# Layer 0's own attention: inner values on both halves of the rows, queries and keys two tiles at a time

## The reference

```python
def _mlp(h, W1, b1, W2, b2):
    return jax.nn.relu(h @ W1.T + b1) @ W2.T + b2
# H, HKV, HD = (16, 4, 64); OH = 64 (width of the hidden layer)
# Wq1 (64, 256), Wq2 (1024, 64): 16 query heads of 64
# Wk1 (64, 256), Wk2 (256, 64): 4 key heads of 64, each for four query heads
# values: x @ Wv.T + bv; causal softmax; the output times Wo (256, 1024)
```

## Time and profile before

| | |
|---|---|
| median of three runs | 2268.53 us |
| time of the profiled execution | 2268.6 us |
| its span, first to last instruction | 2266.8 us |
| TensorE busy in the span | 2013.3 us, 89% |
| VectorE, ScalarE, GpSimd busy | 1339.4, 905.5, 562.2 us |
| mean granted TensorE clock | 0.869 |
| stage of the change | from 386.8 us to about 518 us |
| weights of layer 0's own attention (pack l0a) | 2176 KB, landed 19.4 us after the issue at 3.77 us |

### The profile page before, as it was taken

One profiled execution on the slowest core, in us unless ns is written; L12 is line 12 of the kernel. 1 busy time (PEld: TensorE's weight loads), 2 busy tenths in 40 slices (PEclk: granted clock), 3 DMA queues, 4 the chain that ended last, 5 costly groups with the idle time before them and its releaser, 6 DMA issues.

```text
span 2266.8 us, 57634 instructions
## 1 busy us (share of the span) xinstructions
PE 2013.3 (89%) x22720; PEld 1463.7 (65%) x22720; DVE 1339.4 (59%) x3551; ACT 905.5 (40%) x3432; POOL 562.2 (25%) x1360
## 2 busy tenths in 40 slices
PE   8999999999988898998978888998999999789844
PEld 4899998877566565567866655665644545556623
DVE  6677666765355787445645614886263220678787
ACT  2455554443146565202334523665211111346522
POOL 3566665222011000102345512331000000411111
PEclk9555555999999899899998988999999999889965
DMA  3000001004000001200020000000030000000000
GB/s 139 4 5 5 5 5 66 16 1 185 1 5 5 12 12 53 87 0 24 1 100 37 2 1 8 9 12 1 1 154 0 1 0 0 5 11 12 5 0 16
DMA packets 8026, 57.21 MB, mean 25 GB/s; under 512 B 793, under 2 KB 5249, under 8 KB 5985
## 3 DMA queue, kind: packets, MB, share of 16 engines
q1 hardware_dynamic: 7760, 53.54, 6.2%
HBM read 52.62 MB, written 0.92 MB: 24 GB/s over the span
## 4 chain that ended last, share of the span: by engine, by line
PE 68%; DVE 15%; ACT 7%; issue 6%; POOL 4%; DMA 1%; POOLq 0%; DVEq 0%; SPq 0%; ACTq 0%
PE banks L269 43%; PE banks L274 8%; PE banks L1390 6%; PE banks L963 3%; ACT memory L1011 2%; PE banks L989 2%; DVE memory L1492 2%; PE banks L1543 1%; ACT memory L1417 1%; POOL memory L1449 1%; ACT memory L1424 1%; DVE memory L2835 1%; DVE memory L1498 1%; DVE memory L1273 1%; ACT memory L1256 1%
## 5 line engine op out<-in xcount | busy, mean ns | idle before, releaser
L269 PE MATMUL banks<-memory 128*112 128x256 f32 (+8 forms) x4192 | 1126.1, 424 | 99.2 <-DVE memory L3540 21.8
L269 PEld LDWEIGHTS banks<-memory 128*128 128x128 f32 (+3 forms) x4192 | 699.3, 194 | 434.2 <-issue 279.8
L274 PE MATMUL banks<-memory 112*125 112x112 f32 (+3 forms) x2000 | 301.5, 283 | 75.4 <-DVE memory L850 25.7
L274 PEld LDWEIGHTS banks<-memory 112*125 112x125 f32 (+3 forms) x2000 | 234.7, 170 | 190.9 <-issue 99.5
L1390 PE MATMUL banks<-memory 128*128 128x8 bf16 (+2 forms) x10752 | 306.9, 174 | 14.1 <-DVE memory L1475 1.4
L1390 PEld LDWEIGHTS banks<-memory 128*128 128x128 bf16 x10752 | 295.8, 104 | 25.8 <-POOL memory L1449 23.6
L1011 ACT ACTIVATE memory<-banks,memory 112x375 f32<-112x375 f32 x384 | 215.5, 579 | 26.1 <-DVE memory L1049 26.0
L1049 DVE TENSOR_REDUCE memory<-banks 112x2 f32<-112x750 f32 x192 | 171.1, 934 | 39.2 <-PE banks L963 39.0
L1492 DVE TENSOR_REDUCE memory<-banks 128x48 f32<-128x192 f32 x448 | 122.0, 291 | 61.9 <-PE banks L1390 47.6
L1057 DVE COPY memory<-banks 125x448 f32<-125x448 f32 x192 | 117.0, 620 | 9.5 <-PE banks L274 5.1
L1571 ACT ACTIVATE memory<-memory 112x112 f32<-112x112 f32 x192 | 71.7, 374 | 89.0 <-DVE memory L1592 89.0
(11 more groups left out here) (240 smaller groups left out, 2471.8 us busy)
## 6 DMA issues: line engine op xcount, KB each, us to landing
memory<-in_l2x SPq DMA_DIRECT2D x1, 7680.0 KB, 21.5
memory<-in_l2f SPq DMA_DIRECT2D x1, 7168.0 KB, 20.0
memory<-in_l1f SPq DMA_DIRECT2D x1, 4617.0 KB, 14.5
memory<-in_ctxT SPq DMA_DIRECT2D x24, 187.5 KB
memory<-in_l2f SPq DMA_DIRECT2D x1, 4096.0 KB, 12.9
memory<-in_l3f SPq DMA_DIRECT2D x1, 3073.0 KB, 22.3
memory<-in_l2a SPq DMA_DIRECT2D x1, 3072.0 KB, 18.4
memory<-in_l0f SPq DMA_DIRECT2D x1, 2304.0 KB, 9.2
```

The costliest lines, as they stand in the source:

```text
L269: ins = self.nc.tensor.matmul(out, weights[i], acts[i], start=i == 0, stop=i == n - 1)
L274: return self.nc.tensor.transpose(out, in_, self.ident[0:n, 0:n])
```

## The change

The hidden layers are computed twice: `wq1`, `wk1` and their biases are laid out twice side by side, so that a "hid" matmul fills 128 partitions, with the same 64 values in the lower and in the upper half. The second matrices are split in two halves of their outputs; the first half lies on rows 0 to 63, the other on rows 64 to 127. Queries then take eight matmuls in a row, alternately on the two halves, into two banks; keys four matmuls in the same manner, into two banks. The second "queries" entry of the order goes away, "keys" goes into EVEN and "queries" into ODD. VectorE waits for both banks of a step at once, and takes keys out in two instructions where there was one. Signals for keys count two an item.

```diff
-    EVEN = (("turn", 0, 2), ("sc", 0, 1), ("max", 0, 1), ("exp", 0, 1), ("queries", 0, 0), ("values", 0, 2),
+    EVEN = (("turn", 0, 2), ("sc", 0, 1), ("max", 0, 1), ("exp", 0, 1), ("keys", 0, 0), ("values", 0, 2),
             ("inv", 0, 1), ("y", 0, 3))
-    ODD = (("turn", 1, 2), ("sc", 1, 1), ("max", 1, 1), ("exp", 1, 1), ("keys", 0, 0), ("values", 1, 2),
-           ("queries", 1, 0), ("v", 0, 0), ("hid", 0, -1), ("hid", 1, -1), ("inv", 1, 1))
+    ODD = (("turn", 1, 2), ("sc", 1, 1), ("max", 1, 1), ("exp", 1, 1), ("queries", 0, 0), ("values", 1, 2),
+           ("v", 0, 0), ("hid", 0, -1), ("hid", 1, -1), ("inv", 1, 1))
...
-            k.project(k.bank(bank, 64, S), [w[("wq1", "wk1")[i]][:, j, :] for j in range(KD)],
+            k.project(k.bank(bank, P, S), [w[("wq1", "wk1")[i]][:, j, :] for j in range(KD)],
                       [self.hs[:, i, j, b, :] for j in range(KD)]).then_inc(*s.hid_full.up())
         elif step == "queries":
             PE.wait_ge(*s.hid_ready(2 * b + 1))
-            bank = k.next_bank(("queries", b, i), s.q_ready(2 * b + i + 1))
+            banks = [k.next_bank(("queries", b, h), s.q_ready(2 * b + h + 1)) for h in range(2)]
             for t in range(4):
-                c = 4 * i + t
-                ins = PE.matmul(k.bank(bank, P, 4 * S)[:, t * S:(t + 1) * S], w["wq2"][0:64, c * P:(c + 1) * P],
-                                self.r1[:, 0, :], start=True, stop=True)
-            ins.then_inc(*s.q_full.up())
+                for h in range(2):
+                    rows = slice(64 * h, 64 * h + 64)
+                    ins = PE.matmul(k.bank(banks[h], P, 4 * S)[:, t * S:(t + 1) * S],
+                                    w["wq2"][rows, t * P:(t + 1) * P], self.r1[rows, 0, :], start=True, stop=True)
+                    if t == 3:
+                        ins.then_inc(*s.q_full.up())
         elif step == "keys":
             PE.wait_ge(*s.hid_ready(2 * b + 2))
-            bank = k.next_bank(("keys", b), s.k_ready(b + 1))
-            for t in range(4):
-                ins = PE.matmul(k.bank(bank, P, 4 * S)[:, t * S:(t + 1) * S], w["wk2"][0:64, t * P:(t + 1) * P],
-                                self.r1[:, 1, :], start=True, stop=True)
-            ins.then_inc(*s.k_full.up())
+            banks = [k.next_bank(("keys", b, h), s.k_ready(2 * b + h + 1)) for h in range(2)]
+            for t in range(2):
+                for h in range(2):
+                    rows = slice(64 * h, 64 * h + 64)
+                    ins = PE.matmul(k.bank(banks[h], P, 2 * S)[:, t * S:(t + 1) * S],
+                                    w["wk2"][rows, t * P:(t + 1) * P], self.r1[rows, 1, :], start=True, stop=True)
+                    if t == 1:
+                        ins.then_inc(*s.k_full.up())
...
+            V.wait_ge(*s.q_full(2 * b + 2))
+            for h in range(2):
+                ps = k.bank(k.at["queries", b, h], P, 4 * S).rearrange("p (t s) -> p t s", t=4)
+                V.scalar_tensor_tensor(out=self.q[b % 2][:, 4 * h:4 * h + 4, :], in0=ps, scalar=0.125,
+                                       in1=self.bq2s[:, 4 * h:4 * h + 4].unsqueeze(2).broadcast_to([P, 4, S]),
+                                       op0=ALU.mult, op1=ALU.add).then_inc(*s.q_ready.up())
+        elif step == "keys":
+            if b >= 2:
+                V.wait_ge(*s.sc_full(2 * (b - 1)))
+            V.wait_ge(*s.k_full(2 * b + 2))
+            for h in range(2):
+                V.tensor_tensor(self.kT[b % 2][:, 2 * h:2 * h + 2, :],
+                                k.bank(k.at["keys", b, h], P, 2 * S).rearrange("p (t s) -> p t s", t=2),
+                                self.bias["bk2"][:, 2 * h:2 * h + 2].unsqueeze(2).broadcast_to([P, 2, S]),
+                                ALU.add).then_inc(*s.k_ready.up())
...
+    halves = lambda w: np.concatenate(np.split(w, 2, axis=1), 0)
+    twice = lambda w: np.concatenate([w, w], 0)
...
-        "wq1": inout(f("L0_attn_Wq1").T), "wk1": inout(f("L0_attn_Wk1").T),
-        "wq2": pad(f("L0_attn_Wq2").T),
-        "wk2": pad(np.stack([wk2, wk2], 1).reshape(512, 64).T),
+        "wq1": inout(twice(f("L0_attn_Wq1")).T), "wk1": inout(twice(f("L0_attn_Wk1")).T),
+        "wq2": halves(f("L0_attn_Wq2").T),
+        "wk2": halves(np.stack([wk2, wk2], 1).reshape(512, 64).T),
```

More of the change, by code:

```diff
@@ L1639, in __init__ @@
         take = buffers(Region(k.mem, k.Bm.start, 5000), Region(k.mem, k.after_pack, k.A.start + 22528 - k.after_pack))
-        self.r1, self.bq2s = take(2, S, parts=64), take(8)
+        self.r1, self.bq2s = take(2, S), take(8)
         self.q, self.kT = [take(8, S) for _ in range(2)], [take(4, S) for _ in range(2)]
@@ L1653, in wait_scores @@
         self.nc.tensor.wait_ge(*self.s.q_ready(2 * b + i + 1))
-        self.nc.tensor.wait_ge(*self.s.k_ready(b + 1))
+        self.nc.tensor.wait_ge(*self.s.k_ready(2 * (b + 1)))
     def score(self, b, i, h, j):
@@ L1717, in dve_more @@
             if b:
-                V.wait_ge(*(s.k_full(b) if i else s.q_full(2 * b)))
-            V.tensor_scalar(self.r1[:, i, :], k.bank(k.at["hid", b, i], 64, S),
-                            self.bias[("bq1", "bk1")[i]][0:64, :], 0.0, ALU.add, ALU.max).then_inc(*s.hid_ready.up())
+                V.wait_ge(*(s.k_full(2 * b) if i else s.q_full(2 * b)))
+            V.tensor_scalar(self.r1[:, i, :], k.bank(k.at["hid", b, i], P, S),
+                            self.bias[("bq1", "bk1")[i]], 0.0, ALU.add, ALU.max).then_inc(*s.hid_ready.up())
@@ L1721, in dve_more @@
         elif step == "queries":
[L1722 to L1730, removed]
@@ L1731, in dve_more @@
             if b >= 2:
                 V.wait_ge(*s.sc_full(2 * (b - 1)))
-            V.tensor_tensor(self.kT[b % 2], k.bank(k.at["keys", b], P, 4 * S).rearrange("p (t s) -> p t s", t=4),
-                            self.bias["bk2"].unsqueeze(2).broadcast_to([P, 4, S]), ALU.add).then_inc(*s.k_ready.up())
+            V.wait_ge(*s.q_full(2 * b + 2))
[13 more added lines that the diff above has]
+                                ALU.add).then_inc(*s.k_ready.up())
@@ L3798, in lay_out @@
         "b_lstm": np.concatenate([col(gates(f("L0_attn_b_q"))[:, 0]), col(gates(f("L0_attn_b_k"))[:, 0])], 1),
-        "bq1": pad(f("L0_attn_bq1")[:, None]), "bk1": pad(f("L0_attn_bk1")[:, None]),
+        "bq1": twice(f("L0_attn_bq1")[:, None]), "bk1": twice(f("L0_attn_bk1")[:, None]),
         "bq2": col(f("L0_attn_bq2")), "bk2": np.concatenate([bk2, bk2], 1).T,
```

## The result

The changed kernel took 2253.65 us, median of four runs (2251.78 to 2257.80), beside 2268.51 for the kernel before: a ratio of 0.9936, 95% interval 0.9922 to 0.9950. That is 14.9 us less, where 8.4 were forecast. Two later sets of the same two kernels gave 0.9944 (0.9921 to 0.9966) and 0.9961 (0.9948 to 0.9974). Over all sets the kernel before has 92 runs from 2261.6 to 2277.8 with a median of 2268.5, and the changed one 14 runs from 2251.8 to 2261.4 with 2257.3: 11.2 us less. One set is thus not the size of the change. The three sets of the changed kernel have 2251.8 to 2257.8, 2253.5 to 2256.9 and 2258.4 to 2261.4 us, and against the kernel before in the same set they are 14.9, 15.3 and 8.0 us faster. The third doesn't overlap the other two, so a part of the scatter goes by the set, and the pooled median of 2257.3 lies between two groups.

A forecast was written before the change was run, and what follows sets the result against it. TensorE was taken to bound mid-stage, busy 13.90 of 13.90 us per item. Five periods gaining 6.7 us plus 1.8 at the start made 8.5 off 2268.6 us: 2260.1 us, range 2257.3 to 2264.5.

The forecast's parts named there:

- Pairs on TensorE: Query and key matmuls on alternate halves, per item in mid-stage: 1.46 us in place of 2.85, 1.39 less.
- lower bound: Queries and keys with both halves wholly side by side at the single cadence: 0.89 and 0.45, 1.34 us per item.
- The next limit: Loop through value matmuls, y, scores, masks, exponentials, reciprocal and copies sets the period: 12.57 us, against TensorE's sum of 12.51.
- VectorE's copies fit: Moved query, v and hidden copies, 2.4 us, fit VectorE's 2.62 us idle ahead of the reciprocal in each period.
- Rival B: VectorE becomes the bound, each period late by 0.3–0.5 us, period 12.9–13.1; 2262.6 us, chance 0.2.
- A: Rival: the halves don't overlap with full-width weights, 1 to 3 us gained; 2266.5 us, chance 0.08.
- C: Rival: the clock falls each period at TensorE's wait for copies, period 16.0 us; slower, 2277 us, chance 0.03.
- The single fall near 491 us: One clock fall where the wait grows from 0.55 to about 1.5 us, costing up to 3; 2263 us, chance 0.07.
- Middle and end: Five periods between the masks at 416.26 and 485.75 gain 1.33 us each, 6.7 together; nothing gained behind 485.75.
- the start: From the stage's beginning to the mask of 416.26: 1.8 us gained, between 1.0 and 2.2, first mask 2.0 earlier.
- The rest of the kernel unchanged: Sign expected in the profile after: everything outside the changed attention stage stays as before, adding nothing to the sum.

The follow-up runs named there:

- serial: The changed kernel with all query and key tiles on rows 0 to 63, weights padded with zeros; 2262.99 us, median of ten runs.
- before_again: The kernel before, no edit, traced and timed again; 2268.31 us, stage 136.1 us.
- before_filled_twice: The kernel before with extra v projections into an unread bank, filling two TensorE waits at the stage's start; 2265.75 us, ratio 0.9992.

## Why the prediction was wrong, point by point

- **Pairs on TensorE: right, a little better.** Forecast 1.46 for queries and keys, measured 1.35. The overlap is whole, so the "lower bound" was the value. Why the scores, my row for it, take 0.97 and not 0.89 was not tried; they stand behind the transposes, the queries behind the scores.
- **The next limit: right.** The loop of 12.57 us was read off one passage of the end of the stage, and the period is 12.57. TensorE's own sum is 12.57 − 0.28 = 12.29, not 12.51, and the loop hides the difference.
- **VectorE's copies fit: right.** 0.75 us are left ahead of the reciprocal. Rival B did not come, nor did A (serial shows what it would be) or C: the clock is 1.00 in mid-stage in spite of a wait per item. The single fall near 491 us did not come behind the longer wait (1.61 us at 484.62), but the fall in the wait of 4.37 us, which both kernels have, lasted 6.8 us for 3.4.
- **Middle and end: right in the mechanism.** The 7.4 us of the first pair of traces are 2.2 up to the mask of 416.26, 0.6 from the first period behind it (13.28 us in the changed kernel, with a second fall of the clock at 416.4), 5.3 from four periods at 1.33, and 0.7 given back at the end (32.6 us behind the last of the five for 31.9, with y at half clock). Forecast were 1.8 + 6.7 + 0. VectorE's rows of the changed kernel, to set beside the earlier trace rows:

```profile
414.87 1.14 DVE L1587 TENSOR_TENSOR memory<-banks,memory 112x448 f32<-112x448 f32 x2
428.15 1.16 DVE L1587 TENSOR_TENSOR memory<-banks,memory 112x448 f32<-112x448 f32 x2 [0.21 <-PE banks L1543]
478.45 1.16 DVE L1587 TENSOR_TENSOR memory<-banks,memory 112x448 f32<-112x448 f32 x2 [0.21 <-PE banks L1543]
```

- **The clock in the stage: a step that failed.** The sum priced the kernel before by its one trace: "I take 1.8 us gained at the mask of 416.26, between 1.0 and 2.2", then five periods of 13.90, then nothing. For that pair the start was well sized: 2.2 (31.7 us behind the recurrence before, 29.5 after). One reading in it was wrong: the scores were to "run wholly at half clock, 1.7", but the clock rose at 396.0, ahead of them, and they took 1.04, so the first mask came 2.5 us sooner and not 2.0. But in that trace of before, with 6.8 us at half clock from 408.8 on, part of the loss hid in the wait that comes there in any case. In three other traces the fall comes at 416 to 417 us, at the end of that wait, when TensorE is the bound, and the stage is 3.0 us longer. Of the 3.0, 2.4 lie between the mask that the forecast starts its five periods from and the next one (9.11 us in before_again for 6.72), and 0.7 at the end of the stage, which has 6.8 us at half clock for 3.4:

```profile
417.33 1.14 DVE L1587 TENSOR_TENSOR memory<-banks,memory 112x448 f32<-112x448 f32 x2
426.44 1.16 DVE L1587 TENSOR_TENSOR memory<-banks,memory 112x448 f32<-112x448 f32 x2 [0.21 <-PE banks L1543]
```

  So the usual gain of the stage is 10.6 us (136.1 against 125.5): 2.1 up to the mask, 8.3 in the five periods and 0.3 at the end, for 1.8, 6.7 and 0. I weighed a fall as a risk of the change only; it is a cost of the kernel before, which the changed one pays in two stretches of 3.4 us.
- **Everything behind the stage: the step that put the measured time outside the range.** "The rest of the kernel unchanged" holds for the instructions and was wrong as a forecast of times. The lower end of the range gave the pairs and the later stages 2.4 us together; in the first pair of traces the parts behind the stage differ by 9.9, more than the whole miss, while the stage gave 1.1 less than forecast. The rest is 1682.3 to 1689.4 in nine traces with the serial or old order and 1681.2 to 1688.3 in nine of the others, with means of 1685.6 and 1684.5: a difference far inside 8 us of scatter, which is more than my range's width. The first pair of traces had both ends of it. So the 6.4 us between forecast and measurement are 2.1 in the stage (10.6 for 8.5), 0.6 between that and the pooled 11.2, and 3.7 the scatter between sets (14.9 for 11.2), which no run here explains. By the usual traces the mis-sized term is the stage (8.5 for 10.6 us); by the first pair it is the parts behind the stage, which stood in the sum with nothing and in the range with too little. The pooled median, 2257.3, is the lowest value of my range, and the third set lies inside it. Three runs of before within 1.6 us made me believe in a scatter that 92 runs put at 16.

What stays open: that before_filled_twice has no fall in its start was seen in one trace only; why serial is about 5 us faster than the kernel before; what makes one set of runs differ from the next; and why the falls of the later stages come where they do was not tried.

## What to carry to other kernels

Two K=64 float32 tiles on the two halves of the rows, in two banks, took the time of one here (0.89 us for 16 instructions as for 8); price it at half, and then look for a passage of the old trace in which the next limit already runs alone, since its length can be the new period, as the 12.57 us were here. Before trusting a few microseconds, take several traces of the kernel before: a wait of 2 us in a ramp may or may not drop the clock, and what that costs depends on whether TensorE is the bound when it happens. Compare identical stages of the two traces first; what differs there, and differs as much between two traces of one kernel, is not to be booked to the change.

## What the runs showed of the hardware

- The 16 query instructions with 128 columns of weights each take 0.89 us on alternate halves, as much as 8 on one half; on one half 16 take 1.78.
- Two kinds of pieces take 0.14 to 0.18 us longer behind a piece of another split of rows or columns: transposes 0.91 behind 64-wide hidden layers or values, 0.77 behind 128-wide ones or y; queries 1.07 behind values, 0.89 behind scores. Values have 0.92 behind queries and behind y alike, so not every change of split shows a cost.
- In the start of the stage the granted clock fell from 2.4 to 1.2 GHz behind, or during, waits of 2.08 and 2.21 us, for 6.8, 10.2 or 17 us in the kernels with unpaired tiles. The 2.08 us were followed by a fall in one of four traces of the kernel before, the 2.21 in the other three. In the changed kernel it fell behind waits of 3.03 and 1.67 us for 3.4 us each; its wait of 1.61 us at 484.62 was followed by none until the 4.37 us ten microseconds later:

```profile
405.13 0.70 PE L269 MATMUL banks<-memory 128*128 128x112 f32 x4 [3.03 <-DVE memory L1732]
...
415.05 0.99 PE L1699 MATMUL banks<-memory 112*64 112x112 f32 x16 [1.67 <-issue]
```

The first row is TensorE's timeline of the changed kernel just before the half clock of 406.2 to 409.6, the second before that of 416.4 to 419.9.
